# The feed-forward part's first rows and weights are loaded inside the last attention group

## The reference

```python
def activation_quant(x):
    scale = 127.0 / jnp.clip(jnp.max(jnp.abs(x), axis=-1, keepdims=True), EPS, None)
    return jnp.clip(jnp.round(x * scale), -128.0, 127.0) / scale
def weight_quant(w):
    scale = 1.0 / jnp.clip(jnp.mean(jnp.abs(w)), EPS, None)
    return jnp.clip(jnp.round(w * scale), -1.0, 1.0) / scale
def bitlinear(x, w, b):
    return jnp.einsum('bsd,fd->bsf', activation_quant(x), weight_quant(w)) + b
h = bitlinear(x, w1, b1)              # 256 -> 1024
h = jax.nn.gelu(h, approximate=False)
h = layernorm(h, gamma, beta)
return bitlinear(h, w2, b2)           # 1024 -> 256
...
x = x + jnp.tanh(g_xattn[1]) * _L1_xattn_ref(_layernorm(x, axis=-1), ctx_512, ...)
x = x + jnp.tanh(g_ffn[1]) * _L1_ffn_ref(_layernorm(x, axis=-1), w1, b1, gamma, beta, w2, b2)
```

## Time and profile before

| | us |
|---|---|
| median of 3 runs | 3462.48 |
| lowest, highest | 3459.86, 3468.43 |
| profiled execution, its own time | 3453.07 |
| its span, first to last instruction | 3451.3 |

### The profile page before, as it was taken

How to read it: one execution, slowest core, us unless ns; L and a number is a source line. 1 busy time by engine, 2 the same in 40 slices (tenths; PEclk the granted TensorE clock), 3 DMA queues, 4 the chain that set the end, 5 groups by cost and what they waited for, 6 DMA issues and landing times. The chain is left out here.

```text
span 3451.3 us, 55919 instructions
## 1 busy us (share of the span) xinstructions
PE 2991.1 (87%) x16656; PEld 1994.4 (58%) x16656; DVE 2328.9 (67%) x3226; ACT 1338.7 (39%) x2810; POOL 1560.2 (45%) x1035
## 2 busy tenths in 40 slices
PE   5999879999799999999998999999999999996344
PEld 4777779998555555565565565555556556553123
DVE  5877854445666676686676677667668667664887
ACT  1333322222244344434434434444443443442456
POOL 0000022222454655555655565555555555542566
PEclk9999989999799999999999999999999999998566
DMA  3000010002100000000000000000010100002000
GB/s 107 0 0 0 0 51 5 9 9 53 29 15 20 18 16 15 22 12 19 20 12 22 15 15 16 22 15 16 16 24 7 24 15 13 17 11 69 25 14 23
DMA packets 129556, 70.00 MB, mean 20 GB/s; under 512 B 83566, under 2 KB 123854, under 8 KB 129224
## 3 DMA queue, kind: packets, MB, share of 16 engines
q1 hardware_dynamic: 129288, 66.79, 7.8%
HBM read 56.30 MB, written 10.04 MB: 19 GB/s over the span
## 5 line engine op out<-in xcount | busy, mean ns | idle before, releaser
L1082 POOL TENSOR_TENSOR c_psum<-c_p 120x800 f32<-120x800 f32 (+1 forms) x384 | 751.0, 1961 | 779.1 <-ACT c_p L1300 463.8
L1141 DVE TENSOR_REDUCE c_mneg<-c_m_ps 128x1 fp32r<-128x1452 f32 (+1 forms) x448 | 744.9, 1663 | 413.0 <-PE c_m_ps L1344 412.7
L1300 ACT ACTIVATE c_p<-c_s_ps 120x400 f32<-120x400 f32 (+1 forms) x1536 | 655.1, 508 | 772.7 <-PE c_s_ps L1427 770.1
L1440 PE MATMUL c_o_ps<-c_p,c_val 120*64 120x400 f32 (+1 forms) x3072 | 598.8, 511 | 5.8 <-DVE c_q L1171 5.8
L1426 PE MATMUL c_s_ps<-c_q,c_k 128*120 128x400 f32 (+1 forms) x1536 | 569.2, 371 | 12.3 <-issue 5.6
L1427 PE MATMUL c_s_ps<-c_q,c_k 128*120 128x400 f32 (+1 forms) x1536 | 530.1, 345 | 0.0
L1344 PE MATMUL c_m_ps<-c_k,c_q 64*128 64x484 f32 (+1 forms) x1344 | 324.1, 439 | 100.3 <-DVE c_mneg L1141 70.9
L1426 PEld LDWEIGHTS c_s_ps<-c_q,c_k 128*120 128x120 f32 (+1 forms) x1536 | 278.8, 182 | 171.5 <-issue 158.7
L1073 POOL TENSOR_TENSOR c_rot<-c_psum,c_rs 96x400 f32<-96x400 f32 x256 | 261.0, 1040 | 210.3 <-DVE c_rs L1184 210.2
L1440 PEld LDWEIGHTS c_o_ps<-c_p,c_val 120*64 120x64 f32 (+1 forms) x3072 | 187.0, 136 | 281.4 <-issue 139.4
L1381 PE MATMUL c_s_ps<-c_xt,l_a 128*96 128x400 f32 x1536 | 308.7, 351 | 1.9 <-DVE c_xt L1129 1.9
(11 more groups left out here) (220 smaller groups left out, 4148.1 us busy)
## 6 DMA issues: line engine op xcount, KB each, us to landing
c_rdb<-l_denominators SPq DMA_DIRECT2D x128, 100.0 KB, 2.7
c_kv<-in_ctx SPq DMA_DIRECT2D x32, 360.0 KB
c_q<-c_mneg SPq DMA_DIRECT2D x384, 0.5 KB, 1.9
c_den<-c_oden SPq DMA_DIRECT2D x256, 0.8 KB
x_rows<-in_x SPq DMA_DIRECT2D x4, 800.0 KB
x_spill<-x_rows SPq DMA_DIRECT2D x8, 400.0 KB
c_xa<-x_spill SPq DMA_DIRECT2D x8, 400.0 KB
c_xr<-x_spill SPq DMA_DIRECT2D x32, 100.0 KB
```

Source lines behind the costliest of these rows:

```text
L1082: g.tensor_tensor(psum[0:k, u % 2, :], p[0:k, 2 * u % 4, :], p[0:k, (2 * u + 1) % 4, :], ALU.add).then_inc(psum_ready, 1)
L1141: v.tensor_reduce(mneg[0:n, c, t:t + 1], m_ps[0:n, :, 0:4 * KP], AX.XY, ALU.max, negate=True).then_inc(mneg_ready, 1)
L1300: a.activation(p[0:k, w % 4, i * HALFQ:(i + 1) * HALFQ], s_ps[0:k, (2 * w + i) % 4, 0:HALFQ], ACT.Exp).then_inc(exp_ready, 1)
L1440: mm = pe.matmul(o_ps[i * DL:(i + 1) * DL, 0:HALFQ], val[0:k, j % 2, r, :], p[0:k, w % 4, i * HALFQ:(i + 1) * HALFQ], start=(r == 0), stop ...
```

## The change

CK becomes a constant of the file. The tiles rs and rot of the attention become one shared tile m.rr, whose first 16 KB of each partition are also w1r and w2r (the raw weights of the feed-forward part); xa becomes the first part of a shared tile of 128 partitions and 5 x 256 elements. In the last group, behind the store of its first batch, SP issues w1, w2 and the first 5 tiles of rows (load_early) into these buffers, after waits for the head's last uses of them. Behind the last addition of sums VectorE makes a matrix of ones, reduces |w1| and |w2|, and then, between the steps of the attention's tail, makes the statistics, scales, normalisation and maxima of the first 5 tiles; behind the last add to x it rounds these rows and does two of the three passes over w1. GpSimd gets one power and TensorE one small matmul more in the tail. Each of these VectorE operations waits for the one before it. The attention has four more counters to prime.

The feed-forward part loads no w1 and w2 any more and prepares no first chunk. b1, gamma and beta lie in dead buffers of the attention, so they load behind the barrier; the order is b1, b2, the second chunk, gamma, beta, the first chunk (now only for the residual), and the rest. In front of its loop VectorE keeps the conversion of the identity, the subtraction that makes xq, the third pass over w1, and the copies of the turned rows. It waits for b1 and b2 there.

```diff
-        xa, xr = sb("c_xa", [S, G, D]), sb("c_xr", [S, G, D])
+        xa, xr = m.xa[0:S, 0:G, :], sb("c_xr", [S, G, D])
...
-        rs, rot = sb("c_rs", [HALF, 2, 2 * T]), sb("c_rot", [HALF, 4, 2, T])
+        rs = m.rr[0:HALF, 0:4 * T].rearrange("p (i t) -> p i t", i=2)
+        rot = m.rr[0:HALF, 4 * T:12 * T].rearrange("p (i a t) -> p i a t", i=4, a=2)
...
+                def load_early():
+
+                    sp.wait_ge(q_ps_ready, PRIMED + NG * (H // 2))
+                    sp.wait_ge(rot_ready, PRIMED + NG * H * 2)
+                    sp.dma_start(m.w1r, io["L1_w1T"].rearrange("(k p) n -> p k n", p=128)).then_inc(early_loaded, 16)
+                    sp.dma_start(m.w2r, io["L1_w2T"].rearrange("(k p) n -> p k n", p=128)).then_inc(early_loaded, 16)
+                    sp.wait_ge(xt_ps_ready, PRIMED + NG * KT)
+                    rows_in = io["spill"].rearrange("b s d -> (b s) d").rearrange("(t p) d -> p t d", p=128)
+                    sp.dma_start(m.xa[:], rows_in[:, 0:CK, :]).then_inc(early_loaded, 16)
...
+                        if j == 1 and not more:
+                            load_early()
...
+                g.wait_ge(early_ln, PRIMED + 2 * CK + 1)
+                g.tensor_tensor(erstd[:], eve[:], m.mhalf[:, 0:CK], ALU.pow).then_inc(early_rstd, 1)
...
+                def step(ins):
+                    ins.then_inc(early, 1)
+                    done[0] += 1
+                    v.wait_ge(early, PRIMED + done[0])
+                v.wait_ge(early_loaded, 16 * 3)
+                step(v.memset(eones[:], 1.0))
+                step(v.tensor_reduce(m.wabs[:, 0:1], m.w1r, AX.XY, ALU.add, apply_absolute_value=True))
+                step(v.tensor_reduce(m.wabs[:, 1:2], m.w2r, AX.XY, ALU.add, apply_absolute_value=True))
+                assert done[0] == WSUM
                 invert(B * CH - 1)
+                layernorm_stats(v, lambda j: m.xa[:, j, :], estats, emv, eve, CK, early_ln, 0, m.carrier)
+                v.wait_ge(early_sum, PRIMED + 1)
+                step(v.tensor_scalar(m.wmean[:], m_ps[:, 1, 0:2], 1.0 / (F * D), EPS, ALU.mult, ALU.max))
+                step(v.reciprocal(m.wscale[:], m.wmean[:]))
+                step(v.tensor_scalar(m.wmean[:, 1:2], m.wmean[:, 1:2], m.tg[:, 3:4], None, ALU.mult))
                 normalise(B * CH - 1, 1)
+                v.wait_ge(early_rstd, PRIMED + 1)
+                tiles = slice(0, CK)
+                for j in range(CK):
+                    step(v.tensor_scalar(m.xa[:, j, :], m.xa[:, j, :], emv[:, j, 0:1], erstd[:, j:j + 1], ALU.subtract, ALU.mult))
+                step(v.tensor_reduce(m.xmax[:, tiles], m.xa[:], AX.X, ALU.max, apply_absolute_value=True))
+                step(v.tensor_scalar(m.xmax[:, tiles], m.xmax[:, tiles], EPS, 1.0 / 127.0, ALU.max, ALU.mult))
+                step(v.reciprocal(m.xscale[:, tiles], m.xmax[:, tiles]))
+                step(v.tensor_scalar(m.xdeq[:, tiles], m.xmax[:, tiles], m.wmean[:, 0:1], None, ALU.mult))
                 add_x(B - 1, G - 1, NG - 1)
+                for j in range(CK):
+                    step(v.tensor_scalar(m.xa[:, j, :], m.xa[:, j, :], m.xscale[:, j:j + 1], ROUND, ALU.mult, ALU.add))
+                step(v.tensor_scalar(m.w1r, m.w1r, m.wscale[:, 0:1], ROUND, ALU.mult, ALU.add))
+                step(v.tensor_scalar(m.w1r, m.w1r, -ROUND, 1.0, ALU.add, ALU.min))
                 v.wait_ge(x_added, PRIMED + B)
...
                 sums(B * CH - 1)
+                pe.wait_ge(early, PRIMED + WSUM)
+                pe.matmul(m_ps[:, 1, 0:2], eones[:], m.wabs[:], start=True, stop=True).then_inc(early_sum, 1)
                 pe.wait_ge(od_ready, PRIMED + B * CH)
                 project(B - 1)
...
+                for t, n in ((b1, "L1_ffn_b1"), (b2[:], "L1_ffn_b2")):
+                    sp.dma_start(t, io[n].partition_broadcast(P)).then_inc(b_loaded, 16)
+                load_rows(1)
+                for t, n in ((gamma, "L1_ffn_gamma"), (beta, "L1_ffn_beta")):
+                    sp.dma_start(t, io[n].partition_broadcast(P)).then_inc(loaded, 16)
                 load_rows(0)
-                sp.dma_start(w1r[:], io["L1_w1T"].rearrange("(k p) n -> p k n", p=128)).then_inc(w_loaded, 16)
-                sp.dma_start(w2r[:], io["L1_w2T"].rearrange("(k p) n -> p k n", p=128)).then_inc(w_loaded, 16)
-                for t, n in ((b2, "L1_ffn_b2"), (b1, "L1_ffn_b1"), (gamma, "L1_ffn_gamma"), (beta, "L1_ffn_beta")):
-                    sp.dma_start(t[:], io[n].partition_broadcast(P)).then_inc(loaded, 16)
-                for c in range(1, NCK):
+                for c in range(2, NCK):
                     load_rows(c)
...
                 g.wait_ge(pre_done, PRIMED + 1)
-                deviation(0)
-                g.wait_ge(loaded, 16 * 4)
+                g.wait_ge(loaded, 16 * 2)
...
                 pre(v.memset(mhalf[:], -0.5))
-                first = rows_ahead(0)
-                next(first)
-                next(first)
-                pre(v.memset(ones[:], 1.0))
                 pre(v.tensor_copy(identb[:], m.ident[:]))
-                v.wait_ge(w_loaded, 16 * 2)
-                pre(v.tensor_reduce(wabs[:, 0:1], w1r[:], AX.XY, ALU.add, apply_absolute_value=True))
-                pre(v.tensor_reduce(wabs[:, 1:2], w2r[:], AX.XY, ALU.add, apply_absolute_value=True))
-                v.wait_ge(w_sum, PRIMED + 1)
-                pre(v.tensor_scalar(wmean[:], h_ps[:, 0, 0:2], 1.0 / (F * D), EPS, ALU.mult, ALU.max))
-                pre(v.reciprocal(wscale[:], wmean[:]))
-
-                pre(v.tensor_scalar(wmean[:, 1:2], wmean[:, 1:2], m.tg[:, 3:4], None, ALU.mult))
-                next(first)
-                next(first)
-                next(first)
-                for i, ins in enumerate(quantize(w1r, w1, 0)):
-                    ins.then_inc(w1_ready, 1)
-                    v.wait_ge(w1_ready, PRIMED + i + 1)
-                next(first)
-                v.wait_ge(loaded, 16 * 4)
-                second = quantize(w2r, w2, 1)
+                pre(v.tensor_scalar(xq[:], m.xa[:], -ROUND, None, ALU.add))
+                v.wait_ge(b_loaded, 16 * 2)
+                v.tensor_scalar(w1[:], m.w1r, -1.0, None, ALU.max).then_inc(w1_ready, 1)
+                for k in range(KT):
+                    v.wait_ge(xt_ps_ready, PRIMED + k + 1)
+                    v.tensor_copy(xqt[:, k, :], t_ps[:, 0, 0:CK * P]).then_inc(xt_ready, 1)
+                second = quantize(m.w2r, w2, 1)
...
-                pe.wait_ge(pre_done, PRIMED + 5)
-
-                pe.matmul(h_ps[:, 0, 0:2], ones[:], wabs[:], start=True, stop=True).then_inc(w_sum, 1)
                 turn_rows(0)
-                pe.wait_ge(w1_ready, PRIMED + 3)
+                pe.wait_ge(w1_ready, PRIMED + 1)
```

More of the change, by code:

```diff
@@ L17 @@
 NG = B // G
+CK = 5
 T = G * S
@@ L1524, in phase_l1_ffn @@
         rows = sb("d_rows", [P, NTL, D])
-        w1r, w2r = sb("d_w1r", [128, KT, F]), sb("d_w2r", [128, FT, D])
         w1, w2 = sb("d_w1", [128, KT, F], BF16), sb("d_w2", [128, FT, D], BF16)
-        b1, gamma, beta, b2 = sb("d_b1", [P, F]), sb("d_gamma", [P, F]), sb("d_beta", [P, F]), sb("d_b2", [P, D])
-        ones = sb("d_ones", [128, 128])
+        b1, gamma = (m.cvo[:].rearrange("p h n -> p (h n)")[:, i * F:(i + 1) * F] for i in range(2))
+        beta = m.mqk_all[:].rearrange("p a h n -> p (a h n)")[:, 0:F]
+        b2 = sb("d_b2", [P, D])
         identb = sb("d_identb", [128, 128], BF16)
         mhalf = sb("d_minus_half", [P, CK])
-        wabs, wmean, wscale = sb("d_wabs", [128, 2]), sb("d_wmean", [128, 2]), sb("d_wscale", [128, 2])
+        wmean, wscale = m.wmean, m.wscale
         stats, mv, ve, rstd = sb("d_stats", [P, CK, 6]), sb("d_mv", [P, CK, 2]), sb("d_ve", [P, CK]), sb("d_rstd", [P, CK])
         xn = sb("d_xn", [P, CK, D])
-        xmax, xscale, xdeq = (sb(f"d_x{n}", [P, NTL]) for n in ("max", "scale", "deq"))
+        xmax, xscale, xdeq = m.xmax, m.xscale, m.xdeq
         xq = sb("d_xq", [P, CK, D], BF16)
@@ L1609, in _ @@
                         g.wait_ge(norm_ready, PRIMED + t + 1)
[L1610 removed]
+                        g.tensor_tensor(h1[:, t % RING, :], hg[:, t % RING, :], gamma, ALU.mult).then_inc(gamma_ready, 1)
                         g.wait_ge(gamma_ready, PRIMED + t + 1)
[L1612 removed]
+                        g.tensor_tensor(h1[:, t % RING, :], h1[:, t % RING, :], beta, ALU.add).then_inc(beta_ready, 1)
                     t = tile_at(i, 1)
```

56 lines of the change are left out of this document (35 added, 21 removed).

## The result

The change makes the kernel faster by 0.5%. The median of five runs is 3444.42 us (3438.63 to 3449.62); the kernel before, timed beside it, has 3459.86 (3454.10 to 3468.43). The ratio is 0.995, with a 95% interval from 0.9935 to 0.9965. The fall of the medians is 15.4 us (the interval allows 12 to 22), where the sum had 16.2, and the time forecast was 3446.3. A second measurement, with the kernel unchanged, gave 3442.76 (five runs) against 3458.12 (eleven): 0.9958, from 0.9946 to 0.9971, again 15.4 us.

What follows compares the result with a forecast made beforehand. It took the serial chain from barrier to first h1 (30.9 us) as adding to the time one for one. Terms -18.9 + 2.2 + 0.2 + 0.3 = -16.2 us gave 3446.3 us, range 3439 to 3457.

Steps and rivals of the forecast that it cites:

- The tail in front of the add: Attention's tail up to the add to x: three pieces of early work fit VectorE's waits, cost 0.
- middle piece: Tail, before the product with rdb: statistics, aggregate and scale operations take 4.6 us, done by 3164.9, just fitting; cost 0.
- Rival (c): Attention's tail: the work isn't hidden, up to 2 us lost in all, 3447 to 3449 us; chance 0.04.
- Behind the add: Between add to x and barrier: five roundings and two w1 passes make VectorE last there, cost 2.2 us.
- Barrier to h1: From the barrier to the feed-forward part's first h1: 12.0 us against 30.9, gain 18.9 us.
- The landing: Behind the barrier: b1 with b2, waited for before the last w1 pass, land in 4.5 us (2.5 to 8.6).
- Rival (a): Behind the barrier: the broadcasts land late, at 8.6 us, so the gain is 12.1 and the time 3450.4; chance 0.11.
- The last group: Last attention group: early loads delay the denominator copies queued behind them, cost 0.2 us, between 0 and 4.
- Rival (b): Last attention group: the bulk of early loads holds it up by 2 to 6 us, 3448 to 3452; chance 0.08.
- Rival (d): Last attention group: bulk slows code fetch, starved TensorE's clock falls, kernel slower, 3470 us for 30 us low; chance 0.03.
- Priming of the attention: Before the attention's first load: four more counters to prime, cost 0.3 us.
- The loop: Feed-forward loop: same instructions, period fixed at 51.07 us, cost 0, bounds -2 to +2 us.

Runs made afterwards that it cites:

- e1: Kernel after with early loads kept, but all early VectorE, GpSimd and TensorE work moved back behind the barrier: 3449.37 us, ratio 0.9977 to the kernel before.
- e4: Kernel after with the reduction of w2 done twice in front of the reciprocal: 3439.19 us, one run.
- e2: Kernel after with the two w1 passes moved from behind the last add to x to behind the barrier: 3434.58 us, one run.
- e3: Kernel after with the two w1 passes put into gaps of the tail, before the normalisation and before the add: 3440.31 us, one run.
- e6: Kernel after with the feed-forward part's 30 counters primed in the last attention group, behind the early loads: 3437.52 us, one run.
- e5: Kernel after with a separate semaphore for b1, the last w1 pass waiting for b1 alone: 3450.59 us, one run (3461.64 before).
- e8: Kernel after with w1 passes in the tail's gaps, counters primed in the last group, b1 loaded early: 3431.96 us, ratio 0.992 to the kernel before.
- e10: e8 unchanged, run again on one chip with the unchanged kernel after: 3431.55 us, ratio 0.9924 to the kernel before.
- e7: Kernel after with six more 1 MB transfers between the early loads of w2 and of the rows: 3461.95 us, one run (3461.64 before).
- e9: Kernel after unchanged, timed again: 3442.76 us, ratio 0.9958 to the kernel before.

## Why the prediction was right, point by point

**The tail in front of the add.** Forecast at cost 0 with 0.3 us spare before the reciprocal, hardly any before the product with rdb, and 1.6 before the add. The spare is 0.48, 1.79 and 1.69, and all three distances stayed within 0.13 us. The step was right, and its middle piece was counted too dear: GpSimd's power runs beside VectorE's small operations, as the prediction suspected. In e1, where nothing covers it, VectorE waits only 0.87 us for it. Rival (c) is refuted for this change; e4 shows the condition under which it would have held: a piece longer than its wait.

**Behind the add.** Forecast 2.2 us with VectorE last at the barrier. From the add to the first operation behind the barrier it is 5.46 us instead of 3.24: 2.2. e2 shows that it is the two passes, and e2 and e3 that it need not be paid.

**Barrier to h1.** Forecast 12.0 us from the start of the priming, measured 12.6 (3185.1 to 3197.70; 12.52 from VectorE's first operation, where it had been 30.82). Priming was 2.2 as forecast, and e6 gives it back. The landing was put at 4.5, and 5.3 us pass from the first issue to the landing of b2. That is the one term that was mis-sized, by 0.8. The row it rested on is one transfer of 640 KB; the kernel waits for two, and e5 splits them: 4.1 us for the first, 1.2 more for the second, which starts 0.44 later and, with b1 ahead of it, takes 0.5 to 0.8 longer than alone (e8, e10). From the last weight pass to h1 it is 4.98 us, forecast 5.17. Rival (a), a broadcast of 8.6 us, is refuted: on an empty queue the same 512 KB took 4.1 us from issue to landing (e5), where they took 8.6 behind 2.6 MB.

**The last group.** Forecast 0.2 us, between 0 and 4. From the store of the first batch to the end of the last addition it is 135.05 us after and 135.02 before, so 0.0. The loads landed 5.2, 9.0 and 9.9 us behind their issues, and the reciprocal of the first batch waited 1.31 us, where it had waited 1.30. But the margin is small. The bulk was in 13.8 us behind the store, where the prediction had it in after 12, and the copies of maxima issued meanwhile took up to 7.6 us instead of 1.9. Nothing waited for those, and the reciprocal, at 15.45 us behind the store, came 1.7 us after the bulk. Rival (b) is refuted at 2.64 MB; e7 shows it at 8.6 MB, with a held queue of SP beside the order of landing. Rival (d) is refuted too. With the DMA share at 0.51 the straight-line code of this group ran at a clock of 1.00, with TensorE busy for 16.55 of 18 us (16.52 before). The Trainium skill, "Runtime: NRT & Kernel Launch", Instruction fetch mechanics, calls sequential refill mostly hidden; these rows agree. Only in e7, where TensorE idled behind VectorE, did the clock in this group fall (0.66 from 3050 to 3075, where all others have 1.00).

**Priming of the attention.** Forecast 0.3 us. The 38 increments run from 887.7 to 889.8, and from the barrier to the first load it is 2.3 us instead of 2.1: 0.2. An increment cost a little under 0.06 us here, where it took 0.07 in the feed-forward part.

**The loop.** Forecast 0, from -2 to +2. From h1 to the end it is 244.70 and 243.83 us in two executions of the kernel after and 245.69 in the one of before. Over all executions here, whose loops are the same, it lies between 242.05 and 245.83. So the 1.0 to 1.9 us are not a gain that can be told from the clock's play in this stage, and the period, which the prediction took as fixed, was 50.10 us once, by four matmuls at the higher clock.

**The sum.** From the last addition to h1 it fell by 15.95 us (16.14 in e9) where the forecast was 18.9 - 2.2 = 16.7. With 0.2 for priming, 15.7 to 15.9 are left, and the medians give 15.4 in both measurements. The prediction was right in its parts and not by their cancelling: the largest single error is the 0.8 us of the landing. That the medians agree with the sum within 0.8 us is partly luck, though. Their interval, 12 to 22 us, holds rival (c) as well and reaches down to rival (a), and it is the distances that tell these apart. The time itself was forecast 1.9 us too high: the kernel before came out 2.6 us lower than the median that the forecast started from, and the fall was 0.8 smaller.

## What to carry to other kernels

A barrier between two phases is followed by a fill that nothing covers: transfers into buffers that are dead already can start long before it, and the waits of the serial tail in front of it can hold the work on them, piece by piece, as long as each piece is smaller than its wait. Once that is done, look again at what comes last on each side: here it was VectorE's own overhang at the barrier, the semaphore priming ahead of the first issue, and the second of two small transfers, and moving these as well was worth half as much again (e8). Check too that the bulk is in before the first small transfer behind it is needed: here there were 1.7 us to spare. And read such a gain as a distance between landmarks, since a phase that nobody touched, at another granted clock, moved the span by half as much as the change did.

## What the runs showed of the hardware

- SP can be held at the issue of a transfer. On an empty queue w1 was issued in 0.42 us, and w2 behind it in 0.45 (e7) or 1.42 (after). The six 1 MB transfers that follow in e7 took 16.53 us to issue, some 2.8 us each. The bulk as a whole moved at 0.29 MB a us: 8.6 MB in 29.9 us, from the first issue at 3028.28 to the landing of the rows, 12.4 us behind their issue at 3045.82. Each held issue ended within 0.8 us of the landing of the transfer three places ahead. So SP got only a few transfers ahead of what had landed, and then went at the bulk's pace. Everything behind on SP's queue waited with it, however small. In the kernel after the same is seen in the four row loads behind beta, whose issues took 8.30 us; nothing urgent stands behind them there.
- A broadcast of 512 KB over 128 partitions on an empty queue was there 4.1 us after its issue (e5), one of 128 KB 4.3 and 4.0 us (e8, e10), and the same 128 KB 0.44 us behind the 512 took 4.8 us. A quarter of the bytes saved almost nothing here; having another transfer ahead cost 0.5 to 0.8 us.
- Raising a semaphore cost SP 0.06 to 0.07 us, and 30 of them stood for 2.2 us in front of the first transfer of a phase. In the shadow of another phase they were free.
- One unchanged phase, with TensorE busy for 93 to 94% of the window shown, ended at 436.1 us in one execution and 444.5 in another, at granted clocks of 0.93 and 0.87 in that window.
